# Turning the second MLP projection, and spreading layer 3's attention, in a four-layer kernel

## The reference, cut to what matters

```
layer 0 and 2:  x = x + gelu(h @ w1 + b1) @ w2 + b2            # 512 -> 2048 -> 512
layer 3:        q, k, v = x @ Wq + bq, ctx @ Wk + bk, ctx @ Wv + bv
                scores = einsum('bkgld,bksd->bkgls', q, k) / sqrt(16) + mask
                out = einsum('bkgls,bksd->bkgld', softmax(scores), v)
                y = out @ Wo + bo + x, then a layer norm
```

## Time and profile before

| what | us |
|---|---|
| median of three runs | 3713.37 (3704.5 to 3715.17) |
| time of the profiled execution | 3705.38 |
| its span, first to last instruction | 3703.3 |
| TensorE matmuls busy in the span | 3181.6 (86%) |
| VectorE, ScalarE, GpSimd busy | 1925.4, 1464.4, 881.0 |
| mean granted TensorE clock | 0.913 of full speed |

### The profile page before, as it was taken

The page is one execution under the profiler, slowest core; times in us unless marked ns, Lnnn a source line. Parts: engine busy times, 40 slices in busy tenths (PEclk is TensorE's granted clock), DMA queues, the critical chain, the costliest instruction groups (busy, mean ns, idle before and its releaser), DMA issues. The chain is left out here.

```text
span 3703.3 us, 47771 instructions
## 1 busy us (share of the span) xinstructions
PE 3181.6 (86%) x17231; PEld 2606.8 (70%) x17231; DVE 1925.4 (52%) x3878; ACT 1464.4 (40%) x3347; POOL 881.0 (24%) x891
## 2 busy tenths in 40 slices
PE   3899789797776788999999968999999969788886
PEld 3677468354443388989999868998999868566662
DVE  1444341326875265655565566656666552156653
ACT  1445342111021144455544534446544533155551
POOL 0222310123541231123010431104011320074412
PEclk9999789898887899999999979999999979877777
DMA  3222020100000041014110242104201220111101
GB/s 81 75 66 63 17 91 1 44 12 3 0 12 34 12 138 58 25 44 131 59 48 19 76 124 60 49 18 127 89 25 42 62 91 18 45 61 45 45 3 36
DMA packets 136322, 189.72 MB, mean 51 GB/s; under 512 B 26779, under 2 KB 101404, under 8 KB 136100
## 3 DMA queue, kind: packets, MB, share of 16 engines
q1 hardware_dynamic: 123556, 151.00, 13.5%
q0 software_dynamic: 12544, 35.77, 3.1%
HBM read 167.96 MB, written 15.50 MB: 50 GB/s over the span
## 5 line engine op out<-in xcount | busy, mean ns | idle before, releaser
L63 PE MATMUL l2a<-l_arena,l_arena 128*128 128x400 f32 (+2 forms) x1856 | 649.3, 350 | 36.4 <-DVE l_arena L2459 16.6
L64 PE MATMUL l2a<-l_arena,l_arena 128*128 128x400 f32 (+2 forms) x1856 | 631.1, 340 | 0.0
L65 PE MATMUL l2a<-l_arena,l_arena 128*128 128x400 f32 (+2 forms) x1856 | 631.0, 340 | 0.0
L63 PEld LDWEIGHTS l2a<-l_arena,l_arena 128*128 128x128 f32 (+1 forms) x1856 | 351.5, 189 | 59.1 <-issue 47.8
L64 PEld LDWEIGHTS l2a<-l_arena,l_arena 128*128 128x128 f32 (+1 forms) x1856 | 352.6, 190 | 2.7
L65 PEld LDWEIGHTS l2a<-l_arena,l_arena 128*128 128x128 f32 (+1 forms) x1856 | 351.5, 189 | 2.0
L2148 PE MATMUL l2a<-l_arena,l_arena 121*128 121x384 f32 (+1 forms) x768 | 279.4, 364 | 3.2 <-DVE l_arena L2526 3.2
L2327 ACT ACTIVATE l_arena<-l2a 121x384 fp32r<-121x384 f32 (+1 forms) x208 | 99.7, 479 | 442.8 <-PE l2a L2128 442.8
L2150 PE MATMUL l2a<-l_arena,l_arena 121*128 121x384 f32 (+1 forms) x768 | 264.0, 344 | 0.0
L2149 PE MATMUL l2a<-l_arena,l_arena 121*128 121x384 f32 (+1 forms) x768 | 263.2, 343 | 0.0
L2012 POOL DMA_DIRECT2D p_dram_layer<-l_arena x128 | 62.7, 495 | 726.9 <-DVE l_arena L2526 726.9
(11 more groups left out here) (385 smaller groups left out, 6941.5 us busy)
## 6 DMA issues: line engine op xcount, KB each, us to landing
l_arena<-in_L_xattn_wq_dram SPq DMA_DIRECT2D x32, 512.0 KB, 6.1
l_arena<-in_L_xattn_wk_dram SPq DMA_DIRECT2D x32, 512.0 KB, 7.0
l_arena<-in_L_xattn_wv_dram SPq DMA_DIRECT2D x32, 512.0 KB, 3.8
l_arena<-in_L_xattn_wo_dram SPq DMA_DIRECT2D x64, 256.0 KB, 2.7
l_arena<-ctxT_hi POOLq DMA_DIRECT2D x16, 724.0 KB, 4.5
l_arena<-ctxT_lo POOLq DMA_DIRECT2D x16, 724.0 KB, 6.0
l0mlp_staged<-in_L_xattn_mlp_w_dram SPq DMA_DIRECT2D x16, 512.0 KB, 4.3
l2mlp_staged<-in_L_xattn_w_fc_dram SPq DMA_DIRECT2D x16, 512.0 KB, 4.2
```

The lines of the kernel that those rows point to most:

```text
L63: pe.matmul(out, cut_a(a.hi), cut_b(b.hi), start=start, stop=False)
L64: pe.matmul(out, cut_a(a.hi), cut_b(b.lo), start=False, stop=False)
L65: return pe.matmul(out, cut_a(a.lo), cut_b(b.hi), start=False, stop=stop)
```

## The change

**In the MLP** the second projection is turned: a 128 x 128 piece of w2 is the weights and 400 token columns of hidden features move, so `sums` now holds output features in partitions (4 banks of 400 columns). When a half ends, ACT and DVE copy two sums each into the staging buffers, PE transposes them back (`turn(b)`, 4 transposes for each batch), and DVE adds the result to `X`. The turns of the first half stand among steps 9 and 10 of the second, those of the second half behind the last step. The first projection has three banks in place of four, to make room for a bank for the turned tokens.

```diff
-    STAGES = 4
+    STAGES = KT
+    UP = 3
+    ADD_AT = {(1, 0): [0], (1, 1): [1, 2], (2, 0): [3]}
...
-        banks = psum_banks(nc, own, f"{name}_ps", 4)
-        sums = psum_banks(nc, own, f"{name}_sums", 4)
+        banks = psum_banks(nc, own, f"{name}_ps", UP)
+        sums = psum_banks(nc, own, f"{name}_sums", KT)
+        ps_token = psum_banks(nc, own, f"{name}_token", 1)
...
+        def token_bank(b):
+
+            return ps_token[0] if b <= 4 else banks[b - 5]
...
+                if half > 0 and c == 0:
+                    pe.wait_ge(copied_act, KT // 2 * half)
+                    pe.wait_ge(copied_dve, KT // 2 * half)
+                for m in range(KT):
                     for f in range(CHUNK):
-                        mm = product(pe, sums[b][0:L, :], gT[step % 2], down_w, lambda x: x[:, f, b * L:(b + 1) * L],
-                                     lambda x: x[:, CHUNK * c + f, :],
+                        mm = product(pe, sums[m][:, 0:HALF], down_w, gT[step % 2],
+                                     lambda x: x[:, CHUNK * c + f, m * P:(m + 1) * P], lambda x: x[:, f, :],
                                      start=(c == 0 and f == 0), stop=(c == CHUNKS - 1 and f == CHUNK - 1))
...
+            def turn(b):
+
+                half, c = divmod(b, 4)
+                if c == 0:
+                    pe.wait_ge(copied_act, KT // 2 * (half + 1))
+                    pe.wait_ge(copied_dve, KT // 2 * (half + 1))
+                out = token_bank(b)
+                if b and out is ps_token[0]:
+                    pe.wait_ge(added, b if half == 0 else 4)
+                for m in range(KT):
+                    mm = pe.transpose(out[0:L, m * P:(m + 1) * P], staged[m][:, c * L:(c + 1) * L], k.ident[:])
+                mm.then_inc(token_turned, 1)
...
-                make(step)
+                make(step, 0)
+                if step == CHUNKS + 1:
+                    turn(0)
+                if step == CHUNKS + 2:
+                    turn(3)
+                make(step, 1)
+                if step == CHUNKS + 1:
+                    turn(1)
                 if step > 0:
                     use(step - 1)
+                if step == CHUNKS + 1:
+                    turn(2)
             use(STEPS - 1)
+            pe.wait_ge(activated, CHUNK * STEPS)
+            for b in range(4, B):
+                turn(b)
...
+            def copy_sums(act, steps):
+                act.wait_ge(used, steps)
+                if steps > CHUNKS:
+                    act.wait_ge(token_turned, 4)
+                for m in range(0, KT, 2):
+                    act.activation(staged[m][:, 0:HALF], sums[m][:, 0:HALF], ACT.Copy).then_inc(copied_act, 1)
...
+                if step > 0 and step % CHUNKS == 0:
+                    copy_sums(act, step)
+            copy_sums(act, STEPS)
...
+            def copy_sums(steps):
+                dve.wait_ge(used, steps)
+                if steps > CHUNKS:
+                    dve.wait_ge(token_turned, 4)
+                for m in range(1, KT, 2):
+                    dve.tensor_copy(staged[m][:, 0:HALF], sums[m][:, 0:HALF]).then_inc(copied_dve, 1)
+
+            def add(b):
+                dve.wait_ge(token_turned, b + 1)
+                x = k.X[:, b, :]
+                dve.tensor_tensor(x, x, token_bank(b)[0:L, :], ALU.add).then_inc(added, 1)
...
+                    if half > 0:
+                        for b in ADD_AT.get((c, f), ()):
+                            add(b)
+                if step > 0 and c == 0:
+                    copy_sums(step)
+            copy_sums(STEPS)
+            for b in range(4, B):
+                add(b)
```

```diff
-    TURN = 3
-    BURST = GROUP + TURN + 1
-    NEXT = GROUP
+    TURN = 4
+    SCORES = 3
+    PIECES = 2 * NT3
+    ATTEND = ([22, 23, 25, 27, 29, 31], [2 * GROUP + 5 + i for i in range(PIECES)])
+    KEYS, VALUES = 10, (17, 18, 19, 20, 24, 26)
+    KEYS_COPY = KEYS + KT + 1
+    DIVIDE = 12
+    STACK = [KEYS_COPY + 2 + i for i in range(0, 14, 2)] + [H3 - 1]
...
-        work = psum_banks(nc, own, "work3_", 2)
-        ps_scores = psum_banks(nc, own, "scores3_", 2)
+        work = psum_banks(nc, own, "work3_", 1) * 2
+        ps_scores = psum_banks(nc, own, "scores3_", SCORES)
...
-                    sp.dma_start(dst[:], k.ctxT[part][b].bitcast(F32)).then_inc(cT_loaded, 16)
+                    sp.dma_start(dst[:], k.ctxT[part][b][:, :, 0:S].bitcast(F32)).then_inc(cT_loaded, 16)
...
-                        pe.wait_ge(keys_copied, b)
+                        pe.wait_ge(values_copied, b)
...
-            def project_values(b, j):
-                if j == 0 and b:
-                    pe.wait_ge(values_copied, b)
-                for t in range(KT):
+            def project_values(b, piece):
+                j, half = divmod(piece, 2)
+                if piece == 0:
+                    pe.wait_ge(keys_copied, b + 1)
+                for t in range(KT // 2 * half, KT // 2 * (half + 1)):
...
-                    pe.wait_ge(hi_stacked, PAIRS * b + m + 1)
+                    pe.wait_ge(hi_stacked, 2 * (PAIRS * b + m + 1))
                     pe.wait_ge(lo_stacked, PAIRS * b + m + 1)
                     pe.wait_ge(headed, BLOCKS * (PAIRS * b + m + 1))
-                if h >= 2:
-                    pe.wait_ge(shifted, h - 1)
-                pe.matmul(ps_scores[h % 2][0:L, 0:EVEN], q_heads[b % 2][:, 2 * m + e, g, :], keys[b % 2][:, m, :],
+                if h >= SCORES:
+                    pe.wait_ge(shifted, h - SCORES + 1)
+                pe.matmul(ps_scores[h % SCORES][0:L, 0:EVEN], q_heads[b % 2][:, 2 * m + e, g, :], keys[b % 2][:, m, :],
...
+            def attend(b, e, piece):
+                j, part = divmod(piece, 2)
+                group = 2 * b + e
+                if piece == 0:
...
-                            pe.wait_ge(att_copied, b)
+                            pe.wait_ge(att_copied, Q3 * b)
...
+                    if part == 0:
+                        pe.matmul(ps_att[R * m:R * (m + 1), 0:Q3 * L], values[b % 2][:, j, m, e, :],
+                                  probsT[group % 2][m][:, j, :], start=(e == 0 and j == 0), stop=(e == 1 and j == NT3 - 1))
+                    else:
+                        mm = pe.matmul(ps_sums[R * m:R * (m + 1), 0:Q3 * L], ones[:, e, :], probsT[group % 2][m][:, j, :],
+                                       start=(e == 0 and j == 0), stop=(e == 1 and j == NT3 - 1))
...
+                if b and x + H3 in ATTEND[1]:
+                    attend(b - 1, 1, ATTEND[1].index(x + H3))
+                if b < B and x in ATTEND[0]:
+                    attend(b, 0, ATTEND[0].index(x))
                 if b + 1 < B:
-                    if 0 <= x - NEXT < KT:
-                        project_keys(b + 1, x - NEXT)
-                    if 0 <= x - NEXT - KT < NT3:
-                        project_values(b + 1, x - NEXT - KT)
+                    if 0 <= x - KEYS < KT:
+                        project_keys(b + 1, x - KEYS)
+                    if x in VALUES:
+                        project_values(b + 1, VALUES.index(x))
...
-            def stack_pair(b, m):
-                act.wait_ge(keys_rounded, b + 1)
-                rows = slice(R * m, R * (m + 1))
-                act.activation(keys[b % 2][0:R, m, 0:N3], keysT[rows, :], ACT.Copy)
-                act.activation(keys[b % 2][2 * R:3 * R, m, 0:N3], keysT[rows, :], ACT.Copy).then_inc(hi_stacked, 1)
+            def stack_pair(b, m, copy):
+                if copy == 0:
+                    act.wait_ge(keys_rounded, b + 1)
+                rows = slice(2 * R * copy, 2 * R * copy + R)
+                act.activation(keys[b % 2][rows, m, 0:N3], keysT[R * m:R * (m + 1), :], ACT.Copy).then_inc(hi_stacked, 1)
...
-                    if x == NEXT + KT:
+                    if x == KEYS_COPY:
                         copy_keys(b + 1)
-                    if x == NEXT + KT + 1:
+                    if x == KEYS_COPY + 1:
                         round_keys(b + 1)
-                    if 0 <= x - NEXT - KT - 2 < PAIRS:
-                        stack_pair(b + 1, x - NEXT - KT - 2)
+                    if x in STACK:
+                        stack_pair(b + 1, *divmod(STACK.index(x), 2))
...
+            def copy_attended(b, g):
+                if g == 0:
+                    dve.wait_ge(attended, 2 * (b + 1))
+                columns = slice(g * L, (g + 1) * L)
+                dve.reciprocal(inverse[:, columns], ps_sums[:, columns]).then_inc(inverted, 1)
+                dve.wait_ge(inverted, Q3 * b + g + 1)
+                dve.tensor_tensor(attT[:, g, b * L:(b + 1) * L], ps_att[:, columns], inverse[:, columns], ALU.mult
+                                  ).then_inc(att_copied, 1)
...
+                if b and x - DIVIDE in range(0, 2 * Q3, 2):
+                    copy_attended(b - 1, (x - DIVIDE) // 2)
                 if b + 1 < B:
-                    if x == NEXT + KT + NT3:
-                        copy_values(b + 1)
```

(6 more changed lines are left out.)

96 lines of the change are left out of this document (37 added, 59 removed).

## The result

| | before | after |
|---|---|---|
| median of the runs, us | 3711.84 (4 runs, 3704.50 to 3715.17) | 3607.93 (4 runs, 3600.56 to 3616.32) |
| profiled execution and its span, us | 3705.38, 3703.3 | 3607.46, 3604.8 |
| mean granted clock | 0.913 | 0.928 |

The ratio is 0.9727, with a 95% interval of 0.9706 to 0.9747: faster by 104 us. The forecast was 3614 us, its range 3568 to 3675.

The account below looks back on a forecast made before the run. TensorE alone bounds the MLP; in layer 3 the bound alternates between TensorE and DVE or ACT. From 3705.4 us, less 29.0 (MLPs) and 66.7 (layer 3), 3609.7; with half the median's difference 3614, range 3568 to 3675.

Parts of the forecast that it names:

- a step at 4.37 us: MLP: 24 second-projection matmuls take 4.37 us in place of 5.55, 18.9 us won over 16 steps.
- turns 2.4: MLP: the first half's transposes are new on TensorE's full path, 0.15 us each, 2.4 us lost, their waits nothing.
- tail 4.9: MLP: last matmul to last add takes 4.9 us in place of 2.9, 2.0 us lost.
- copies and three banks at nothing: MLP: copies that free `sums` run under step 9's `make`, and ACT frees three banks early enough; no cost.
- the ends: Layer 3, once: last division 0.9 later, values behind the key copy 0.6, context loads 0.6; 2.1 us lost together.
- factor and half clock: Layer 3 batch: 33.7 us times 1.09 for what the method omits, plus 2.1 for half-clock heads, makes 38.8.
- the attend piece: Layer 3, heads 5 to 10 and 20 to 31: each half attend call costs TensorE 0.745 us, half of 1.49.
- The sign I gave: Layer 3, profile after: single heads at x = 5 to 10 take about 1.2 us each.
- A: Layer 3: three engines overlap wholly, no half clock beyond the first heads, 33.7 us a batch, 3572 us; chance 0.15.
- B: Layer 3: the waits move and almost nothing is won, a batch of 46 us, 3671 us; chance 0.18.
- C: Layer 3: TensorE's half clock holds through the batch, 53.3 us a batch, 3729 us, slower; chance 0.05.
- D: MLP: the turn does not shorten the matmuls, with a 128-column load each; excluded by `make`'s rows.

Follow-up runs that it names:

- calls in a row: The kernel after with whole attend calls in three heads running (22 to 24, and 5 to 7 of the next batch) in place of spread halves: 3635.78 us, ratio 0.9795.
- two banks: The kernel after with two score banks in place of three, everything else as it is: 3609.53 us, ratio 0.9738.
- the added projections: The kernel after with the last batch projecting its own keys and values once more, into a bank nobody reads: 3599.91 us, ratio 0.9705.

## Why the prediction was right, point by point

**The MLP.** Predicted 29.0 us for both, measured 14.8 + 15.3 = 30.1 in the traces and 0.74% (27.5 us) by the kernel with this part alone. Its terms: a step at 4.37 us, measured 4.35; turns 2.4, measured 1.7, with no wait; tail 4.9, measured 4.8; copies and three banks at nothing, which the unbroken step 9 bears out. The turns were taken too dear since the 4.02 us of the earlier trace rows were partly at half clock (mean granted clock 0.67 in them); in after the same 32 transposes take 2.77 us at clock 1.00, 0.087 each, and 0.087 x 1.28 = 0.11 is what was measured. Measured, the terms would make 19.2 - 1.7 - 1.9 = 15.6 for layer 0; the 14.8 is less mainly because in this trace it was 11.2 us from the first `make` matmul to the first `sums` matmul, before 10.3. The Trainium skill's rule on the issue gap ("TensorE: Matmul & The Clock Gate", section "Back-to-back issue gap") gave 17.9 us where the rows gave 18.9; the step now takes 1.20 us less, 19.2 for 16 steps, on the side of the rows.

**Layer 3.** Predicted 38.8 us a batch and 310 from first to last score, measured 38.4 and 307.0; with the ends 68.3 won (72.1 + 0.3 - 4.1) where 66.7 were forecast. The sum came out nearly right, but not by its own terms, so the closeness is partly luck:

| heads | predicted | batch 3 | batch 4, clock 1.00 | what was off |
|---|---|---|---|---|
| 0 to 4 | 4.4 | 3.7 | 3.7 | full clock, and ACT the bound |
| 5 to 10 | 7.7 | 9.2 | 9.2 | a piece costs 0.97, not 0.745 |
| 11 to 19 | 10.0 | 11.1 | 9.7 | in batch 3 half clock at 17 and 18 |
| 20 to 31 | 11.6 | 13.3 | 14.4 | the same piece, and 1.4 that is not explained |
| factor and half clock | 5.1 | | | |
| sum | 38.8 | 37.3 | 36.9 | |

Half clock in the third stretch comes back in the fourth, all but 0.4 us.

The mis-sized term is the attend piece. I took half of 1.49 us, the distance from the call to what follows it. In the timeline of after:

```profile
3340.54 0.51 PE L2965 MATMUL turned<-ident,probs 100*121 100x100 f32 x3
3340.99 0.88 PE L2980 MATMUL att<-probsT,values 121*32 121x400 f32 x8
3341.79 0.41 PE L2957 MATMUL scores<-keys,q_heads 96*100 96x364 f32 x1
...
3343.24 0.41 PE L2957 MATMUL scores<-keys,q_heads 96*100 96x364 f32 x1
```

Heads with a piece follow at 1.45 us (3341.79 to 3343.24), 0.97 more than a bare head; a whole call adds 2.12 - 0.48 = 1.64 (calls in a row), 0.82 for each half. So the call itself was 0.15 us dearer than I read, from the turn before it: in after's timeline an attend matmul starts 0.20 us behind the start of the last transpose, a score 0.05. Halving adds 0.3 a call, 1.8 us a batch. The 12 pieces make 2.7 us more than my sum. With them and full clock at heads 0 to 4 it would be 33.7 + 2.7 - 0.7 = 35.7, so 1.2 of the 36.9 are left for handing over, where I had put 3.0 (the factor 1.09) and 2.1 for half clock. The factor covered the piece; a factor fitted on the kernel before cannot say what it covers. The sign I gave, heads 5 to 10 at about 1.2 us each, failed for the same reason (1.45).

DVE's four divisions were right: 0.78 and 0.26 us, taken as 0.78 and 0.25, at heads 12 to 18.

**Half clock.** I put it at heads 0 to 4 and at two pieces behind them. It came at 17 and 18, behind the wait at 16 and 17 (single microseconds of after):

```profile
3354.00:3355.00 1.00, 0.44 (x4) 0.19 (x2) 0.96 (x5) 0.90 (x2) 0.83 (x2) 1.00 0.00 0
3355.00:3356.00 1.00, 0.70 (x4) 0.50 (x5) 1.00 (x5) 0.48 (x1) 1.00 (x1) 1.00 0.00 0
3356.00:3357.00 1.00, 0.91 (x6) 0.76 (x7) 1.00 (x3) 1.00 (x4) 1.00 (x1) 1.00 0.00 0
3357.00:3358.00 1.00, 1.00 (x7) 0.94 (x6) 0.96 (x5) 0.96 (x4) 1.00 (x1) 0.50 0.00 0
```

TensorE was busy 0.44 and 0.70 of two microseconds, and by 3357 had 1.2 GHz. It does not come in every batch: batch 4 kept 1.00. At heads 0 to 4 I had taken the half clock from rows in which no attend piece stood in the heads just ahead; now pieces stand right up to head 31, and the clock there is 1.00. That the pieces are the reason was not tried by itself.

**The ends.** Predicted 2.1 us lost, measured 4.1 behind the last score less 0.3 at the opening. From the last attend matmul to the end of the last division it was 4.1 us in place of 3.3, so 0.8 for the term of 0.9; the values waited 0.65 us for the key copy at the start (0.6). No row had priced the context loads (0.6), and no loss shows: from the issue of the first part to the first keys matmul 11.3 us, 12.3 before. What I missed is that in this run the last batch ends at half clock, so that the 12 last transposes and the first pieces behind them do too: 77.2 us behind the last score, against 71.5 with two banks and 72.7 with the added projections, where the clock was back by then.

**What carries the gain.** I held the third bank and the turn at four to be what makes the sum fair, together. The runs part them: the bank is worth nothing, the turn's fourth head 3.1 us a batch. The distance between whole calls is worth 3.3, halving them 1.4, the split division 2.1. Each is the price of one step back from after, in one trace, and the last two don't show in the times of the runs; together 9.9 of the 11.6 us between the two kernels' batches (49.1 and 37.5), though such prices need not add. What the place of ACT's key copies and of the keys and values calls is worth was not tried by itself.

**The rivals.** A (33.7 a batch) fell: even at clock 1.00 a batch takes 37.0. B (46) fell: a batch takes 37.5, and even with the turn at three heads, the nearest to what it feared, one took 38.8 to 44.8. C is not the layer, but the second half of its last batch. My argument against it, that TensorE busy at half clock with attend work gets full clock back, fell there: 18.06 of 18.20 us busy, attend pieces among them, and the clock stayed at 0.50. D was excluded and stayed so.

## What to carry to other kernels

Where several engines hand a head from one to the next, put the extra work of the busiest engine at a distance from its like, and leave the consumer far enough behind that the chain fits (here four heads of 0.65 us for a chain of about 1.9); a third buffer bought nothing here. Price a piece by the distance between two repeats with it, less that without it, not by the distance to the next operation. Where the busiest engine's clock falls behind a gap, look for the stretch that lost work, such as a last round without a next one to prepare; work that nobody reads keeps the clock there, though here its gain stayed within the scatter.
